# A selective scan in a Mamba and mixture-of-experts layer: GpSimd adds the two states of every second unit, TensorE adds one tile instead of two

## The chip, the cores and the metric

The kernel runs on one core of one Trainium2 chip. The metric is the device time of one launch in microseconds. Three runs of the kernel before took 6356.14, 6356.43 and 6366.62 us; their median is 6356.43 us. All tensors of the part that matters here are 32-bit floats.

## The reference, cut to what matters

```python
# per sequence, x: (512 tokens, 256); D_INNER = 512 channels, D_STATE = 16
xz = x @ in_proj_w.T;  u, res = split(xz, 2)
u = silu(conv_b + causal 4-tap convolution of u)
dt, B, C = split(u @ x_proj_w.T)
delta = softplus(dt @ dt_proj_w.T + dt_proj_b);  A = -exp(A_log)
def step(h, t):
    h = exp(delta_t[..., None] * A) * h + delta_t[..., None] * B_t[:, None, :] * u_t[..., None]
    y = einsum('bdn,bn->bd', h, C_t)         # sum over the 16 states
y = (y + u * D_skip) * silu(res);  m = y @ out_proj_w.T
# then: layer norm, an additive attention with l2 norms, a GELU feed-forward
# of width 1024, layer norms; then top-2 routing to 8 experts with a capacity,
# the experts' matmuls, and the weighted sum with a residual
```

It is applied to 32 sequences of 512 tokens. Only the sum over the states in `y` is computed in another way by the change.

## The kernel before, in words

There are three phases one after the other: `attention_phase` (the Mamba layer, the attention, the feed-forward and the routing, for 32 sequences), `expert_phase` and `combine_phase`. The change touches the first alone, which takes about 5.4 of the 6.4 milliseconds.

**Units.** The 512 channels of a sequence are four blocks of 128 partitions. A unit is one block with two of the 16 states, so a sequence has 32 units, k = 0 to 31 (`NU`), eight to a block. For unit k:
- ScalarE computes the decays `dA` = exp(delta * A), one activation for each of the two states (`decay`, L740);
- VectorE multiplies `du` = delta * u with the row B into `drive` (`drive`, L1077, 128x1024), and runs the recurrence over dA and drive into the tile `st` (`recur`, L1104, one instruction over 2 x 512 columns);
- GpSimd multiplies `st` in place with the row C (`times_c`, L528, 128x1024);
- TensorE adds the two halves of `st` into the bank `Y` by two matmuls with the identity (`add`, L912). Each 32-bit matmul is two records in the trace, so a unit is four records of L912. A block opens with one matmul that puts u * D_skip into Y (L909), and ends with VectorE's product of Y with the gate, `gate`, L1083.

`st` has four buffers (`RING`): the recurrence of unit k waits (semaphore `scan_sum`) until TensorE has added unit k-4. B_rows has two buffers and C_rows four; SyncE loads both in one order, and a load of C_rows waits for the product of four units before.

**Side stages.** Beside the scan of sequence b, every engine works on three side stages: `pre` of sequence b+1 (norm, input projection, convolution, delta), `post` of b-1 (output projection, attention, first feed-forward matmul) and `late` of b-2 (second feed-forward matmul, norms, routing, scatter to the experts). Each engine has one instruction stream in a fixed order. That order is written out by tables: a unit has three slots, so a sequence has 96, and each `at = iter((...))` lists, for the pieces of one side stage on one engine, behind which slot each comes. `run_slots` puts the scan's part of a slot first and the pieces behind it. An engine whose next piece waits does nothing else meanwhile.

Two points of a sequence serve as marks below. *idx* is L1260 on VectorE: the table of expert slots of sequence b-2 is ready, between the recurrences of units 13 and 14; GpSimd waits for it to issue eight indirect DMAs (L615). *The gate* is the L1083 of the last block of the sequence before, in front of the recurrence of unit 1: it waits for TensorE's add of that sequence's unit 31, which follows GpSimd's product of unit 31.

## Time and profile before

| | |
|---|---|
| median of three runs | 6356.43 us |
| profiled execution, its own time | 6355.55 us |
| its span | 6353.8 us |
| TensorE busy (matmul) | 5465.8 us, 86% |
| VectorE busy | 5085.4 us, 80% |
| GpSimd busy | 4353.1 us, 69% |
| ScalarE busy | 3682.9 us, 58% |
| mean granted TensorE clock | 0.933 |

The busy shares are over the whole span. The first phase takes most of it, and the steady part of that phase (1000 to 5000 us) is where the shares are read below. "Idle before" is time that an engine spent waiting in front of an instruction, with what ended the wait behind the arrow. The time of 6355.55 us is 1.75 us longer than the span, for what lies around it.

### The profile page before, as it was taken

The numbers are of one execution on the slowest core, as the hardware profiler recorded it, in microseconds if no ns is written. First come the engines' busy times: TensorE is split into PE (matmuls) and PEld (weight loads), VectorE is DVE, ScalarE is ACT, GpSimd is POOL, SyncE is SP. The second block draws the span as 40 slices with busy tenths as digits, with TensorE's granted clock in tenths as the row PEclk, the third lists the DMA queues.
The fourth block names the chain that finished last, engine by engine and source line by source line (L and its number), as shares of the span: only waits on it lengthen the run. The fifth ranks groups of instructions, "written<-read, shape, count | busy, mean of one in ns | idle before, by whom it ended". The sixth has DMA issues, their size and how long they took to land. (4 is left out here: it accounts for less than half of the span.)

```text
span 6353.8 us, 72231 instructions
## 1 busy us (share of the span) xinstructions
PE 5465.8 (86%) x17152; PEld 3037.6 (48%) x17152; DVE 5085.4 (80%) x6700; ACT 3682.9 (58%) x6370; POOL 4353.1 (69%) x2996
## 2 busy tenths in 40 slices
PE   3788988888889898888888888898888988749997
PEld 1344444444444454454444444444454454436663
DVE  4898898898988898888898899889998888712226
ACT  3566666666666666666666666666666666421113
POOL 2677777777777777777777777777777777622223
PEclk8899999999999999999999999999999999869999
DMA  7666666666666666666666666666666666403337
GB/s 263 228 227 232 227 233 226 215 230 227 230 229 225 216 226 220 226 229 226 231 229 216 212 222 223 218 216 218 219 223 217 221 226 216 156 25 123 119 111 324
DMA packets 470519, 1349.76 MB, mean 212 GB/s; under 512 B 54495, under 2 KB 161888, under 8 KB 468592
## 3 DMA queue, kind: packets, MB, share of 16 engines
q1 hardware_dynamic: 437904, 1270.68, 59.0%
q10 hardware_dynamic: 13664, 39.47, 1.7%
q0 software_dynamic: 18432, 34.17, 1.5%
q14 instruction: 374, 3.06, 0.2%
q8 instruction: 145, 2.38, 0.1%
HBM read 1206.71 MB, written 154.66 MB: 214 GB/s over the span
## 5 line engine op out<-in xcount | busy, mean ns | idle before, releaser
L528 POOL TENSOR_TENSOR st<-st,C_rows 128x1024 f32<-128x1024 f32 x1024 | 2478.0, 2426 | 519.8 <-DVE st L1104 510.4
L1104 DVE TENSOR_TENSOR_SCAN st<-dA,drive 128x1024 f32<-128x1024 f32 x1024 | 2338.5, 2284 | 247.7 <-PE y L912 110.7
L912 PE MATMUL y<-st,ident 128*128 128x512 f32 x4096 | 1970.8, 619 | 163.4 <-POOL st L528 161.1
L740 ACT ACTIVATE dA<-delta,a_neg 128x511 f32<-128x511 f32 x2048 | 1368.0, 712 | 699.9 <-DVE st L1104 691.8
L912 PEld LDWEIGHTS y<-st,ident 128*128 128x128 f32 x4096 | 794.2, 199 | 1183.9 <-issue 878.2
L1077 DVE TENSOR_TENSOR drive<-du,B_rows 128x1024 f32<-128x1024 f32 x1024 | 1259.9, 1230 | 101.1 <-DVE du L1072 21.7
L881 PE MATMUL pre_bank<-e_abs,in_w 128*128 128x512 f32 x1024 | 579.3, 706 | 84.7 <-DVE u L1054 78.0
L860 PE MATMUL post_bank<-d_w,gT 128*128 128x256 f32 x2048 | 471.8, 388 | 35.8 <-issue 35.0
L860 PEld LDWEIGHTS post_bank<-d_w,gT 128*128 128x128 f32 x2048 | 397.9, 195 | 136.1 <-issue 82.7
L615 POOL DMA_INDIRECT expert_in<-tb,idx x256 | 271.1, 1059 | 267.0 <-DVE idx L1260 195.5
L1419 POOL DMA_INDIRECT rank_rows<-O,dest_i x128 | 124.5, 973 | 381.8 <-issue 381.8
L881 PEld LDWEIGHTS pre_bank<-e_abs,in_w 128*128 128x128 f32 x1024 | 211.4, 219 | 343.1 <-issue 204.2
L1054 DVE SCALAR_TENSOR_TENSOR u<-pre_bank,conv_w,u 128x511 f32<-128x511 f32 (+2 forms) x384 | 285.6, 744 | 36.3 <-ACT u L685 27.3
L984 PE MATMUL post_bank<-F,d_w 128*128 128x512 f32 x512 | 246.1, 626 | 3.6 <-ACT gT L811 2.0
L852 PE MATMUL post_bank<-ident,tb 128*128 128x128 f32 x768 | 117.3, 302 | 143.6 <-ACT tb L643 113.1
L860 PE MATMUL post_bank<-F,gT 128*128 128x256 f32 x512 | 157.8, 477 | 90.6 <-ACT F L792 90.6
L1371 PE MATMUL bank<-XT,w 128*128 128x512 f32 x512 | 227.7, 598 | 5.3 <-ACT XT L1396 5.3
L1381 PE MATMUL bank<-w,I 128*128 128x256 f32 x1024 | 228.6, 382 | 3.3 <-issue 3.3
L984 PE MATMUL pre_bank<-F,d_w 128*128 128x512 f32 x512 | 230.2, 592 | 0.0
L860 PE MATMUL pre_bank<-out_w,u 128*128 128x256 f32 x1024 | 226.3, 379 | 2.5 <-issue 2.5
L1404 ACT ACTIVATE I<-bank 128x512 f32<-128x512 f32 x64 | 38.2, 597 | 316.5 <-PE bank L1371 316.5
L1469 DVE TENSOR_SCALAR O<-bank,w_slot 128x256 f32<-128x256 f32 x128 | 53.1, 477 | 210.3 <-PE bank L1381 210.3
(211 smaller groups left out, 8217.6 us busy)
## 6 DMA issues: line engine op xcount, KB each, us to landing
B_rows<-bc_rows SPq DMA_DIRECT2D x1024, 512.0 KB, 3.7
C_rows<-bc_rows SPq DMA_DIRECT2D x1024, 512.0 KB, 4.9
rank_rows<-zeros SPq DMA_DIRECT2D x32, 1024.0 KB, 9.0
rows<-rank_rows SPq DMA_DIRECT2D x32, 1024.0 KB, 18.6
expert_in<-gT ACTq DMA_DIRECT2D x11, 1536.0 KB, 25.5
X<-expert_in SPq DMA_DIRECT2D x32, 528.0 KB, 3.8
xin<-in_x SPq DMA_DIRECT2D x32, 512.0 KB, 6.8
xn_rows<-xin SPq DMA_DIRECT2D x32, 512.0 KB, 3.4
```

Source lines behind the costliest of these rows:

```text
L528: pool.tensor_tensor(tile[:, :, :], tile[:, :, :], bc[1][k % ROWS[1]][:, :, :], ALU.mult)\
L615: pool.indirect_dma_start(out=xe_dram, out_offset=bass.IndirectOffsetOnAxis(ap=idx[:, tile, choice:choice + 1], axis=0), in_=tb_wide[:, ti ...
L740: return act.activation(dA[k % 2][:, j, 1:L], delta[par][:, c, 1:L], ACT.Exp, scale=a_neg[:, c, n:n + 1])
L860: last = pe.matmul(banks[tile // 2][:, (tile % 2) * D:(tile % 2 + 1) * D], srcT[:, c, tile * P:(tile + 1) * P], w[:, c, :], start=c == 0, ...
L881: last = pe.matmul(RB[m % 2][:, :], in_w[:, c, m * P:(m + 1) * P], xT[:, c, :], start=c == 0, stop=c == KD - 1)
L912: last = pe.matmul(Y[:, :], ident[:, :], st[k % RING][:, j, :], start=False, stop=pair == CU - 1 and j == 1)
L984: last = pe.matmul(FB[j % 4][:, :], d1_w[:, c, j * P:(j + 1) * P], F[:, c, :], start=c == 0, stop=c == KD - 1)
L1054: dve.scalar_tensor_tensor(late, RB[c % 2][:, 0:L - 1 - j], conv_w[:, c, 2 - j:3 - j], late, ALU.mult, ALU.add).then_inc(pre_dve.did(f"con ...
L1077: dve.tensor_tensor(DR[:, :, :], DU[:, :].unsqueeze(1).to_broadcast([P, 2, L]), bc[0][k % ROWS[0]][:, :, :], ALU.mult).then_inc(scan_in.di ...
L1104: dve.tensor_tensor_scan(st[k % RING][:, :, :].rearrange("p a l -> p (a l)"), dA[k % 2][:, :, :].rearrange("p a l -> p (a l)"), DR[:, :, : ...
L1371: last = pe.matmul(MB[m][:, 0:BLK], w1[e][:, c, m * P:(m + 1) * P], XT[n % 2][:, c, :], start=c == 0, stop=c == KD - 1)
L1381: last = pe.matmul(OB[tile // 2][:, (tile % 2) * D:(tile % 2 + 1) * D], I[n % 2][:, c, tile * P:(tile + 1) * P], w2[e][:, c, :], start=c = ...
```

## The change: every second unit is added in halves by GpSimd first

For even k, `times_c` issues a second instruction behind its product: it waits for that product, adds half 1 of `st` to half 0 (128x512) and only then signals `scan_hc`. TensorE's `add` does one matmul for such a unit instead of two. Odd units are as before. All tables of the side stages have new numbers; of these the diff shows four.

```diff
+        def PAIRED(k):
+            return k % 2 == 0
...
+        scan_pair = Steps(sem("scan_pair"), [k for k in range(NU) if PAIRED(k)])
...
-                    pool.tensor_tensor(tile[:, :, :], tile[:, :, :], bc[1][k % ROWS[1]][:, :, :], ALU.mult)\
+                    product = pool.tensor_tensor(tile[:, :, :], tile[:, :, :], bc[1][k % ROWS[1]][:, :, :], ALU.mult)
+                    if not PAIRED(k):
+                        product.then_inc(scan_hc.did(k), 1)
+                        return
+                    product.then_inc(scan_pair.did(k), 1)
+                    pool.wait_ge(*scan_pair.at(k, b))
+                    pool.tensor_tensor(tile[:, 0, :], tile[:, 0, :], tile[:, 1, :], ALU.add)\
                         .then_inc(scan_hc.did(k), 1)
...
@@ gpsimd @@
             def post(b, par, more):
-                at = iter((13, 19, 22, 34, 37, 41, 53, 53, 61, 70))
+                at = iter((11, 22, 22, 36, 40, 46, 54, 55, 61, 70))
...
             def late(b):
-                at = iter((0, 1, 18, 20, 22, 27, 29, 43, 43, 45, 45, 45, 45, 48, 51))
+                at = iter((5, 7, 21, 23, 25, 25, 32, 44, 45, 46, 46, 46, 46, 46, 51))
...
-                    for j in range(2):
+                    halves = (0,) if PAIRED(k) else (0, 1)
+                    for j in halves:
                         last = pe.matmul(Y[:, :], ident[:, :], st[k % RING][:, j, :], start=False,
-                                         stop=pair == CU - 1 and j == 1)
+                                         stop=pair == CU - 1 and j == halves[-1])
...
@@ tensor @@
             def late(b):
-                at = iter((0, 10, 10, 13, 38, 38, 45))
+                at = iter((0, 7, 10, 11, 36, 40, 43))
...
@@ vector @@
             def late(b):
-                at = iter((13, 18, 18, 18, 40, 40, 42))
+                at = iter((15, 18, 21, 21, 40, 40, 41))
```

**GpSimd around idx.** In the kernel before, from the product of unit 11 to that of unit 15 (gT is the attention's `li`; the DMAs wait for idx):

```order
L528 TENSOR_TENSOR st<-st,C_rows 128x1024 [waits scan_h]
L565 REGISTER_ALU
L541 TENSOR_TENSOR gT<-gT,row_lni_g 128x1024 [waits post_act]
L526 REGISTER_ALU
L527 REGISTER_ALU [waits C_loaded0]
L528 TENSOR_TENSOR st<-st,C_rows 128x1024 [waits scan_h]
L568 REGISTER_ALU
L545 TENSOR_TENSOR gT<-gT,row_lni_b 128x1024 [waits post_pool]
L527 REGISTER_ALU [waits C_loaded1]
L528 TENSOR_TENSOR st<-st,C_rows 128x1024 [waits scan_h]
L612 REGISTER_ALU
L615 DMA expert_in<-tb,idx 16384x264 [waits late_dve]
```

In the changed kernel, from the product of unit 13 to that of unit 15:

```order
L532 TENSOR_TENSOR st<-st,C_rows 128x1024 [waits scan_h]
L622 REGISTER_ALU
L625 DMA expert_in<-tb,idx 16384x264 [waits late_dve]
L625 DMA expert_in<-tb,idx 16384x264
L531 REGISTER_ALU [waits C_loaded2]
L532 TENSOR_TENSOR st<-st,C_rows 128x1024 [waits scan_h]
L537 REGISTER_ALU
L538 TENSOR_TENSOR st<-st 128x512 [waits scan_pair]
L625 DMA expert_in<-tb,idx 16384x264 x5
L578 REGISTER_ALU
L555 TENSOR_TENSOR gT<-gT,row_lni_b 128x1024 [waits post_pool]
L531 REGISTER_ALU [waits C_loaded3]
```

The wait for idx still stands directly behind the product of unit 13. The addition of row_lni_b has moved from in front of it to behind it, and the product of unit 14 now comes behind two DMAs instead of six.

**VectorE at the feed-forward's norm.** Before, between the recurrences of units 5 and 6 (the form SCALAR_TENSOR_TENSOR of L1104 is the recurrence; the scale r_late of L1188 comes from GpSimd), from the norm's aggregation on:

```order
L1041 BN_AGGR mv_late<-stat_late 128x2 x3
L1186 REGISTER_ALU
L1188 SCALAR_TENSOR_TENSOR post_bank<-post_bank,mv_late,row_ln_g 128x256 [waits late_pool]
L1188 SCALAR_TENSOR_TENSOR post_bank<-post_bank,mv_late,row_ln_g 128x256 x3
L1191 REGISTER_ALU
```

In the changed kernel, the same place:

```order
L1052 BN_AGGR mv_late<-stat_late 128x2 x3
L1112 REGISTER_ALU
L1115 SCALAR_TENSOR_TENSOR st<-dA,drive 128x1024 [waits scan_sum,scan_in,scan_exp]
L1088 TENSOR_TENSOR drive<-du,B_rows 128x1024 [waits scan_h,B_loaded1]
L1197 REGISTER_ALU
L1199 SCALAR_TENSOR_TENSOR post_bank<-post_bank,mv_late,row_ln_g 128x256 [waits late_pool]
```

A whole recurrence and a drive now stand between what GpSimd computes r_late from and what uses it.

**ScalarE at the norm of h.** Before, from the first decay of unit 5 to the second (the normalisation of h waits for GpSimd's h_shift, the one of L656 for x_m):

```order
L740 ACTIVATE dA<-delta,a_neg 128x511 [waits scan_h]
L758 ISA
L643 ACTIVATE h<-h,shift,r 128x256 [waits post_pool]
L643 ACTIVATE h<-h,shift,r 128x256 x3
L740 ACTIVATE dA<-delta,a_neg 128x511
```

In the changed kernel, from the second decay of unit 7 to the first of unit 8:

```order
L750 ACTIVATE dA<-delta,a_neg 128x511
L686 ISA
L687 ISA [waits pre_pe]
L688 COPY e_abs<-pre_bank 128x512 [waits pre_dve]
L689 COPY e_abs<-pre_bank 128x512
L768 ISA
L653 ACTIVATE h<-h,shift,r 128x256 [waits post_pool]
L653 ACTIVATE h<-h,shift,r 128x256 x3
L749 REGISTER_ALU
L750 ACTIVATE dA<-delta,a_neg 128x511 [waits scan_h]
```

The wait for h_shift no longer stands between the two decays of unit 5; it has moved two and a half units back.

## Rows read from the trace of the kernel before

**Rows 1.** Windows: length, busy time and instructions of each engine, PEclk, DMA share, GB/s
```profile
1000.00:5000.00 4000.00, 3540.93 (x11064) 1937.47 (x11062) 3559.84 (x4441) 2600.66 (x4464) 3064.52 (x1994) 0.94 0.66 223
2028.10:2117.20 89.10, 78.47 (x204) 36.74 (x203) 77.71 (x70) 58.32 (x81) 74.88 (x42) 0.92 0.74 251
2117.20:2200.90 83.70, 73.97 (x270) 45.98 (x270) 74.03 (x120) 52.23 (x111) 55.52 (x44) 0.95 0.57 189
2200.90:2285.60 84.70, 75.50 (x208) 36.66 (x208) 78.04 (x72) 58.62 (x82) 73.67 (x42) 0.97 0.78 264
```

**Rows 2.** One line's instructions, 1000 to 5000 us: idx, and who waited
```profile
L1260 DVE TENSOR_SCALAR idx<-slot_f x24: 170/171/172, 1010.7 to 4933.0; 128x8 uint32<-128x8 f32 x24
...
  POOL expert_in L615: 144.8, 24
```

**Rows 3.** Groups by line, 1000 to 5000 us: busy us, mean ns, idle before
```profile
L528 POOL TENSOR_TENSOR st<-st,C_rows 128x1024 f32<-128x1024 f32 x752 | 1820.4, 2427 | 323.0 <-DVE st L1104 318.2
L1104 DVE TENSOR_TENSOR_SCAN st<-dA,drive 128x1024 f32<-128x1024 f32 x752 | 1717.5, 2284 | 185.1 <-PE y L912 83.0 <-ACT dA L740 45.1 <-issue 26.1
L912 PE MATMUL y<-st,ident 128*128 128x512 f32 x3004 | 1431.3, 614 | 73.0 <-POOL st L528 71.1
```

**Rows 4.** Waits of VectorE, 1000 to 5000 us: total us, times, longest
```profile
DVE st L1104 <- PE y L912: 83.0, 64, 2.9
DVE st L1104 <- ACT dA L740: 45.1, 58, 3.3
DVE post_bank L1188 <- POOL r_late L472: 36.4, 23, 1.6
DVE tb L1159 <- PE post_bank L860: 34.3, 16, 3.3
...
DVE gT L1134 <- PE post_bank L860: 11.6, 12, 1.0
DVE cum L1240 <- PE post_bank L1015: 10.6, 12, 1.3
```

**Rows 5.** Timeline of TensorE: start us, us, operation [idle before]
```profile
2078.81 1.09 PE L852 MATMUL post_bank<-ident,tb 128*128 128x128 f32 x8 [2.34 <-ACT tb L643]
2081.03 3.78 PE L912 MATMUL y<-st,ident 128*128 128x512 f32 x4 [1.13 <-POOL st L528]
...
2143.85 5.31 PE L912 MATMUL y<-st,ident 128*128 128x512 f32 x12
```

**Rows 6.** Windows: the four microseconds behind that idle time
```profile
2080.00:2084.00 4.00, 2.97 (x4) 1.43 (x5) 3.81 (x3) 2.95 (x5) 4.00 (x3) 0.50 0.77 271
```

**Rows 7.** Groups by line, GpSimd, 1000 to 5000 us: its short tensor_tensor
```profile
L482 POOL TENSOR_TENSOR shift<-shift,r 128x4 f32<-128x4 f32 x70 | 17.0, 242 | 5.5
```

**Rows 8.** Groups by line, GpSimd, 2028.9 to 2112.6 us: idx to unit 31
```profile
L528 POOL TENSOR_TENSOR st<-st,C_rows 128x1024 f32<-128x1024 f32 x18 | 44.5, 2481 | 10.7 <-DVE st L1104 10.7
L615 POOL DMA_INDIRECT expert_in<-tb,idx x8 | 8.5, 1068 | 8.8 <-DVE idx L1260 6.9 <-issue 1.9
```

**Rows 9.** Timeline of GpSimd
```profile
2028.96 1.11 POOL L615 DMA_INDIRECT expert_in<-tb,idx  x1 [6.94 <-DVE idx L1260]
...
2051.13 6.99 POOL L528 TENSOR_TENSOR st<-st,C_rows 128x1024 f32<-128x1024 f32 x3
...
2091.53 3.26 POOL L528 TENSOR_TENSOR st<-st,C_rows 128x1024 f32<-128x1024 f32 x1 [1.32 <-DVE st L1104]
...
2109.81 2.71 POOL L528 TENSOR_TENSOR st<-st,C_rows 128x1024 f32<-128x1024 f32 x1 [2.79 <-DVE st L1104]
```

**Rows 10.** Timeline of VectorE: idx, the gate, two waits behind it
```profile
2027.88 0.17 DVE L1260 TENSOR_SCALAR idx<-slot_f 128x8 uint32<-128x8 f32 x1
...
2117.27 0.68 DVE L1083 TENSOR_TENSOR u<-y,g 128x512 f32<-128x512 f32 x1
...
2140.70 2.29 DVE L1104 TENSOR_TENSOR_SCAN st<-dA,drive 128x1024 f32<-128x1024 f32 x1 [3.34 <-ACT dA L740]
...
2148.49 1.67 DVE L1188 SCALAR_TENSOR_TENSOR post_bank<-post_bank,mv_late,row_ln_g 128x256 f32<-128x256 f32 x4 [1.58 <-POOL r_late L472]
```

More of the change, by code:

```diff
@@ L370, in pre @@
             def pre(b, par):
-                at = iter((2, 16, 52, 64, 95))
+                at = iter((8, 37, 70, 71, 95))
                 yield next(at)
@@ L410, in post @@
             def post(b, par, more):
-                at = iter((4, 52))
+                at = iter((2, 68))
                 yield next(at)
@@ L425, in late @@
             def late(b):
-                at = iter((38, 58))
+                at = iter((31, 51))
                 yield next(at)
@@ L463, in _ @@
                                pattern=[[1, P]], channel_multiplier=-1).then_inc(consts, 1)
-            for steps in (pre_pool, scan_hc, post_pool, late_pool):
+            for steps in (pre_pool, scan_pair, scan_hc, post_pool, late_pool):
                 steps.credit(pool)
@@ L502, in pre @@
             def pre(b, par):
-                at = iter((11, 16, 67, 69, 70, 73))
+                at = iter((12, 17, 67, 67, 77, 89))
                 yield next(at)
@@ L660, in pre @@
             def pre(b, par):
-                at = iter((10, 14, 17, 17, 19, 19, 25, 36, 43, 43, 48, 55, 59, 59, 59, 60, 61, 62, 65, 66, 69, 92))
+                at = iter((14, 14, 17, 19, 21, 29, 34, 37, 42, 47, 47, 53, 53, 61, 64, 64, 65, 65, 67, 68, 71, 94))
                 def junk(tile):
@@ L755, in post @@
             def post(b, par, more):
-                at = iter((12, 20, 35, 35, 35, 35, 37, 53, 64, 73, 76, 86, 95))
+                at = iter((20, 23, 28, 32, 38, 38, 38, 54, 67, 80, 80, 92, 95))
                 yield next(at)
@@ L814, in late @@
             def late(b):
-                at = iter((22, 25, 25, 30, 36, 42))
+                at = iter((26, 26, 28, 32, 37, 42))
                 yield next(at)
@@ L864, in pre @@
             def pre(b, par):
-                at = iter((20, 25, 25, 25, 36, 38, 46, 46, 47, 49, 52, 52, 55, 55))
+                at = iter((16, 16, 27, 30, 36, 41, 41, 46, 46, 51, 51, 53, 55, 55))
                 yield next(at)
@@ L922, in post @@
             def post(b, par, more):
-                at = iter((1, 2, 24, 26, 26, 44, 48, 54, 61, 67, 76, 78, 83, 84, 88))
+                at = iter((0, 1, 18, 27, 33, 49, 52, 56, 63, 63, 78, 88, 88, 93, 94))
                 for half in range(2):
@@ L1044, in pre @@
             def pre(b, par):
-                at = iter((20, 28, 33, 39, 82, 88, 95))
+                at = iter((22, 33, 37, 39, 85, 95, 95))
                 for c in range(KI):
@@ L1086, in gates @@
             def gates(b, par):
-                at = iter((30, 56, 77))
+                at = iter((28, 54, 78))
                 for c in range(KI - 1):
@@ L1117, in post @@
             def post(b, par, more):
-                at = iter((2, 11, 11, 27, 31, 44, 49, 58, 68))
+                at = iter((2, 10, 11, 25, 26, 46, 51, 63, 68))
                 yield next(at)
```

## The prediction

> **What bounds the kernel now.** I read the busy shares first, then one period of the sequence loop, then who waits for whom. The reader should see that the first phase repeats one pattern: idx comes 24 times from 1010.7 to 4933.0 us [rows 2], so a sequence takes 3922.3 / 23 = 170.5 us. Such a period holds, by 1000 to 5000 us [rows 1], 151.7 us of VectorE (89.0%), 150.9 of TensorE (88.5%), 130.6 of GpSimd (76.6%) and 110.8 of ScalarE. No engine is full. The recurrence on VectorE, 2284 ns [rows 3], waits for the other three, and its waits are the time to be won: for TensorE's add 83.0 us, for ScalarE's decays 45.1, for GpSimd's r_late 36.4, for TensorE's side matmuls 34.3, 11.6 and 10.6 [rows 4]. Over 23.5 sequences (752 units of 32, [rows 3]) that is 5.9 us per sequence for TensorE, 1.9 for ScalarE and 1.5 for GpSimd.
>
> I cut the period at two marks. From idx to the gate the traced sequence takes 2117.2 - 2028.1 = 89.1 us, the next one 84.7; from the gate to idx 83.7 [rows 1, 10]. Over the 24 sequences the first part goes from 84.6 to 89.5 us with a mean of 87.3, the second from 80.3 to 88.7 with a mean of 83.2. The quick first part had a granted clock of 0.97, the slow one 0.92 [rows 1]: TensorE makes the difference between them.
>
> **TensorE's part of the change.** It loses one matmul for each of 16 units per sequence, two records each. Twelve records in a row take 5.31 us at full clock [rows 5], so 0.43 us each with the tail taken off (0.44 by plain division): 16 x 2 x 0.43 = 13.8 us per sequence, 440 us in all. None of it is on the path by itself. What it can give back is VectorE's wait for TensorE, 5.9 us per sequence, and a share of ScalarE's.
>
> **GpSimd's part.** It gains 16 additions of 128x512 per sequence. No row has this form. The bounds are the product of twice the width, 6.99 us for three, so 2.33 each [rows 9], and the 128x4 tensor_tensor, 0.24 us [rows 7]. I take the straight line between them, 0.24 + 508 x (2.36 - 0.24) / 1020 = 1.30 us, since the length grows with the columns and 512 lies in the middle. The wait for its own product adds the 0.08 us that the dependent L482 shows in front of it (5.5 us over 70, [rows 7]). With the overlap of two independent instructions lost, 1.4 us each; 22.4 us per sequence. GpSimd then has 153 us of work in 170.5, more than VectorE. Waiting behind the addition are the next product, all side pieces of GpSimd, and SyncE's load of C_rows four units on, with the B_rows load behind it in the same queue.
>
> [...]
>
> **Where it binds: from idx to the gate.** GpSimd's wait for idx stands directly behind the product of unit 13 in both kernels. From the first DMA behind it to the end of the product of unit 31, 2028.96 to 2109.81 + 2.71 = 2112.52, it took 83.6 us [rows 9], of which 10.7 us were waits for the recurrence [rows 8]. Its own work was 72.9 us, with the 0.9 and 0.35 us by which products stretch beside some of VectorE's work (3.26 and 2.71 against 2.36, [rows 9]). Now nine additions (units 14 to 30) come in, 9 x 1.4 = 12.6, and the addition of row_lni_b that was in front of idx, 2.3 us: 72.9 + 12.6 + 2.3 = 87.8 us with no wait. Before it lie 0.9 us from idx to the first DMA (2028.05 to 2028.96, [rows 9, 10]); behind it TensorE's two matmuls of unit 31, 1.8 us. So the gate comes no earlier than 90.5 us behind idx, against 87.3 now: +3.2 us per sequence. With the additions at the lower bound (0.24 + 0.08) this is 80.8 and GpSimd doesn't bind; at the upper (2.36 + 0.08) it is 99.9.
>
> VectorE's recurrences do not stop in between for long: the four buffers let them run up to four units ahead, some 15 us. But gate and recurrence of unit 1 stand behind unit 31's sum, and there the lag is collected. This is where the gain on TensorE in the same part is lost.
>
> **From the gate to idx.** Here GpSimd was busy 55.5 of 83.7 us [rows 1]; seven additions make it 65, so it has room. VectorE was busy 74.0. What goes: the 3.34 us wait for the decays of unit 5 [rows 10] stood behind ScalarE's wait for h_shift, which is now two and a half units later; the 1.58 us for r_late [rows 10] is covered by a recurrence and a drive, 3.5 us. In the mean over the sequences the two are worth 1.9 + 1.5 us. Half of TensorE's 5.9 us falls into this part; I take 1.9 of 2.9 as gone, and give 0.3 back for the new places where TensorE waits for x_normed early. Sum: 83.2 - 5.0 = 78.2 us. What is late next in this part is the chain of h_sum, h_aggr and h_shift, which starts at the gate.
>
> **The sum.** 90.5 + 78.2 = 168.7 us against 170.5, -1.8 us; 31 periods give -56 us. From the profiled execution, 6355.6 us: 6355.6 - 56 = 6300 us; the median of the runs before is 0.9 us above that execution, which I leave out. The other two phases do not change.
>
> **Rivals.**
> *GpSimd doesn't bind (faster by far).* If the additions are cheap, or overlap more than I grant, the first part becomes what it is when TensorE is in time, 84.7 us: 84.7 + 78.2 = 162.9, -7.6 x 31 = -236, 6120 us; with an addition of about 0.9 us all told, 9 x 0.5 less than mine, it is 86.0 + 78.2 = 164.2, 6160. For it: the quick sequences. Against: 15 us of new work in a part where 10.7 were free.
> *GpSimd binds and nothing is won behind the gate (slower).* The gate is late, so GpSimd comes into the next part already behind, h_shift and r_late come later, and VectorE's waits there stay as they are: 90.5 + 83.2 = 173.7, +3.2 x 31 = +99, 6455 us. For it: GpSimd at 153 of 170 us, and every wait of it now delays products. It decides if the part from gate to idx stays over 82 us. Against: GpSimd's 28 us of idle time in that part.
> *The clock takes it back (no change).* [...] TensorE with 13.8 us less to do stands still more often. If the mean clock falls from 0.94 to 0.88, its work at full clock, 150.9 x 0.94 - 13.8 = 128 us, takes 146 us, hardly less than 151: VectorE's waits for it stay, the period stays at 170.5, 6356 us. [...] Against: the new idle time lies in pieces of under a microsecond behind every second unit, and the clock stayed at 0.97 in the quick stretch, where TensorE was idle for 9 of 85 us [rows 1].
> [...]
>
> **How the numbers follow.** The forecast has 0.43, GpSimd not binding 0.17, the slow case 0.27, the clock 0.13. The measurement tells 0.2% (12.7 us, 0.4 us per sequence) from no change. The forecast's own range is 6250 to 6350, nearly all of it faster (0.37, same 0.04, slower 0.02); the first rival 0.17 faster; the second 0.25 slower, 0.02 same; the clock 0.07 same, 0.03 and 0.03. That makes faster 0.57, same 0.13, slower 0.30. The range must reach into both sides: from 6165, which leaves out the cheapest additions, to 6455, the slow case's own value; the dearest additions (99.9 + 78.2 = 178.1, 6592 us) lie beyond it.
>
> **What would show it.** The addition's row near 1.3 us x 512. TensorE's L912 with 3072 records in place of 4096, its busy share near 82%. GpSimd near 90% in the first phase, with hardly any wait for the recurrence from idx to the gate; the gate at 90 to 91 us behind idx. VectorE's wait at the gate appearing as a new row, its wait for r_late gone, for the decays under half. I am wrong if the first part is under 88 us (then the additions or the stretches are cheaper than taken), or the second over 82 (then the new places don't give what I read from them).

## The result, and the profile after

The changed kernel takes 6554.3 us (median of 4 runs, 6549.3 to 6563.0) against 6358.5 (4 runs): a ratio of 1.031 with a 95% interval of 1.029 to 1.033. The forecast was 6300 us and its range ended at 6455. Profiled span: 6550.2 us.

Windows of the changed kernel, columns as in [rows 1]: the first phase, then one sequence cut at idx and at the gate.

```profile
1000.00:5000.00 4000.00, 3328.58 (x9967) 1807.42 (x9968) 3542.67 (x4306) 2580.86 (x4388) 3413.16 (x2296) 0.87 0.65 216
2105.20:2201.40 96.20, 80.27 (x216) 41.08 (x214) 81.10 (x71) 60.10 (x82) 84.87 (x51) 0.84 0.70 238
2201.40:2281.60 80.20, 65.08 (x227) 38.48 (x226) 74.57 (x120) 53.20 (x112) 65.39 (x51) 0.92 0.58 196
```

Over the sequences of this window the period is 176.1 us for 170.5. The first part (idx to gate) has a mean of 96.1 for 87.3, the second (gate to idx) 80.0 for 83.2. TensorE's granted clock is down from 0.94 to 0.87.

Groups by line, 1000 to 5000 us, columns as in [rows 3]: GpSimd's product and addition, TensorE's sum.

```profile
L532 POOL TENSOR_TENSOR st<-st,C_rows 128x1024 f32<-128x1024 f32 x727 | 1751.8, 2415 | 154.7 <-DVE st L1115 152.1
...
L538 POOL TENSOR_TENSOR st<-st 128x512 f32<-128x512 f32 x363 | 460.2, 1268 | 28.5
...
L923 PE MATMUL y<-st,ident 128*128 128x512 f32 x2184 | 1197.0, 677 | 159.1 <-POOL st L532 121.2 <-POOL st L538 36.9
```

GpSimd's wait for the recurrence is halved, from 318 us in [rows 3] to 152, as new work fills it; TensorE's wait for GpSimd is more than doubled, from 71 to 158.

The pieces of the attention that are named below, in the order in which one needs the other: ssk (sums of squares of the keys, TensorE, then VectorE), the product with w_g (VectorE), G (TensorE) and ssg (VectorE), t (VectorE), t_li (t plus the earlier `li`, GpSimd), its transpose (TensorE) and the copies F (ScalarE), fl (TensorE's matmuls with fl_w), s_sum (fl plus h, VectorE), s_normed (ScalarE) and its transpose sT (TensorE). asg is the routing's assignment of tokens; xp_w is the product whose copy xd leads over dt to delta and so to the decays.

Waits of VectorE, columns as in [rows 4]. L1177 is s_sum (L1166 in the code before), L1164 ssg, L1155 the product of gT with w_g, L1094 the gate.

```profile
DVE tb L1177 <- PE post_bank L870: 114.3, 23, 5.7
DVE st L1115 <- PE y L923: 53.5, 41, 2.5
DVE ssg L1164 <- PE post_bank L971: 37.7, 23, 3.4
DVE gT L1155 <- PE post_bank L961: 34.5, 18, 3.5
DVE gT L1155 <- issue: 17.4, 5, 3.5
DVE u L1094 <- PE y L923: 16.0, 15, 1.8
...
DVE st L1115 <- ACT dA L750: 11.3, 30, 0.6
```

What [rows 4] had at the top is down (83.0 to 53.5 for the sum, 45.1 to 11.3 for the decays, r_late's 36.4 gone, the 34.3 at t, L1159, down to 7.3). But there are new waits at side pieces, all in the first part: 114.3 + 37.7 + 34.5 + 17.4 = 204 us, 9.0 per sequence (for the 17.4 the profile names no releaser). One of these is the longest single wait of the sequence. Timeline of VectorE, changed kernel: t, and s_sum after it.

```profile
2138.23 1.65 DVE L1170 SCALAR_TENSOR_TENSOR tb<-post_bank,rk,row_pr_b 128x256 f32<-128x256 f32 x4
...
2152.37 1.29 DVE L1177 TENSOR_TENSOR tb<-post_bank,h 128x512 f32<-128x512 f32 x2 [5.25 <-PE post_bank L870]
```

Between the two lies a chain over three engines. GpSimd's t_li ran from 2140.92, TensorE's transpose at 2143.33, ScalarE's copies F at 2145.93, TensorE's fl at 2147.03: 12.5 us from the end of t. On VectorE t stands at slot 63 where it was at 58, while s_sum stayed at 68. That is two recurrences between them in place of three, and VectorE waits for the rest. Part of this wait is TensorE's clock. Timeline of TensorE at fl, and the window over it:

```profile
2147.03 5.22 PE L870 MATMUL post_bank<-fl_w,F 128*128 128x256 f32 x16 [1.73 <-ACT F L807]
```

```profile
2147.00:2152.00 5.00, 4.97 (x16) 4.18 (x17) 0.13 (x1) 4.78 (x6) 5.00 (x3) 0.69 0.58 174
```

After idle times of 3.51 us in front of the transpose and 1.73 us in front of fl the mean granted clock over fl was 0.69: 0.50 in each microsecond from 2147 to 2150 us, 0.95 in the next and 1.00 from 2151 on. fl's 16 matmuls took 5.22 us. In the mean they take 5.3 us here, at a granted clock of 0.65 to 0.71 in each of the 23 sequences, and 3.7 in the kernel before, where it is 1.00 over all 24.

### The profile page after: what moved, and what is told of

It reads as the page before. It is cut to its first block and busy times, and to the rows that moved or that the text cites. A ratio compares the mean times of both kernels' runs of the same rounds, so it can differ in the third digit from the quotient of the medians.

```text
span 6550.2 us, 71204 instructions
## 1 busy us (share of the span) xinstructions
PE 5330.4 (81%) x16128; PEld 2945.1 (45%) x16128; DVE 5212.2 (80%) x6700; ACT 3759.7 (57%) x6430; POOL 4984.3 (76%) x3508
## 5 line engine op out<-in xcount | busy, mean ns | idle before, releaser
L923 PE MATMUL y<-st,ident 128*128 128x512 f32 x3072 | 1688.2, 680 | 271.4 <-POOL st L532 178.4
L750 ACT ACTIVATE dA<-delta,a_neg 128x511 f32<-128x511 f32 x2048 | 1353.2, 712 | 834.3 <-DVE st L1115 810.8
L923 PEld LDWEIGHTS y<-st,ident 128*128 128x128 f32 x3072 | 630.4, 214 | 1048.1 <-issue 618.9
L538 POOL TENSOR_TENSOR st<-st 128x512 f32<-128x512 f32 x512 | 649.0, 1268 | 40.2
L891 PE MATMUL pre_bank<-e_abs,in_w 128*128 128x512 f32 x1024 | 597.7, 723 | 68.1 <-ACT e_abs L689 38.3
L891 PEld LDWEIGHTS pre_bank<-e_abs,in_w 128*128 128x128 f32 x1024 | 228.7, 235 | 378.8 <-issue 237.4
L862 PE MATMUL post_bank<-ident,tb 128*128 128x128 f32 x768 | 147.6, 355 | 262.0 <-ACT tb L653 150.3
L862 PEld LDWEIGHTS post_bank<-ident,tb 128*128 128x128 f32 x768 | 119.0, 183 | 355.8 <-ACT tb L653 198.3
L919 PE MATMUL y<-u,d_diag 128*128 128x512 f32 x256 | 196.5, 860 | 100.2 <-DVE u L1094 100.2
L995 PE MATMUL post_bank<-F,d_w 128*128 128x512 f32 x512 | 232.7, 597 | 1.5 <-ACT F L814 1.5
```

The lines of the kernel that those rows point to most:

```text
L538: pool.tensor_tensor(tile[:, 0, :], tile[:, 0, :], tile[:, 1, :], ALU.add)\
L750: return act.activation(dA[k % 2][:, j, 1:L], delta[par][:, c, 1:L], ACT.Exp, scale=a_neg[:, c, n:n + 1])
L862: last = pe.transpose(banks[c][:, tile * P:(tile + 1) * P], src[:, tile, c * P:(c + 1) * P], ident[:, :])
L891: last = pe.matmul(RB[m % 2][:, :], in_w[:, c, m * P:(m + 1) * P], xT[:, c, :], start=c == 0, stop=c == KD - 1)
L923: last = pe.matmul(Y[:, :], ident[:, :], st[k % RING][:, j, :], start=False, stop=pair == CU - 1 and j == halves[-1])
L995: last = pe.matmul(FB[j % 4][:, :], d1_w[:, c, j * P:(j + 1) * P], F[:, c, :], start=c == 0, stop=c == KD - 1)
```

## The experiments

Times are given as ratios to the kernel before, measured in the same session; 1% is 64 us and the intervals are about 0.2% to either side. Parts and periods are means over the sequences of 1000 to 5000 us. "Old" and "new places" are the tables of before and of the change.

| run | ratio, 95% interval | us | first part | second part | clock |
|---|---|---|---|---|---|
| before | 1 | 6353 to 6374 | 87.3 | 83.2 | 0.94 |
| changed | 1.031 [1.029, 1.033] | 6554 | 96.1 | 80.0 | 0.87 |
| e1, new places alone | 1.038 [1.036, 1.040] | 6612 | 97.2 | 80.8 | 0.92 |
| e2, pairs alone | 1.025 [1.022, 1.027] | 6531 | 92.1 | 84.3 | 0.89 |
| e3, both matmuls | 1.042 [1.039, 1.044] | 6639 | 98.3 | 80.2 | 0.91 |
| e4, short addition | 1.018 [1.016, 1.021] | 6492 | 95.3 | 79.5 | 0.88 |
| f1, s_sum later | 1.044 [1.041, 1.047] | 6637 | 98.1 | 81.2 | 0.86 |
| f2, three steps later | 1.054 [1.051, 1.057] | 6700 | 100.4 | 80.7 | 0.86 |
| f3, pairs from unit 22, old places | 1.020 [1.018, 1.023] | 6485 | 88.7 | 86.5 | 0.91 |
| f5, du first | 1.041 [1.038, 1.043] | 6613 | 95.5 | 83.2 | 0.86 |
| g3, tail of the chain later | 1.025 [1.024, 1.027] | 6515 | 94.5 | 80.5 | 0.88 |
| g5, old chain, pairs | 1.032 [1.030, 1.034] | 6553 | 92.2 | 84.0 | 0.88 |
| g6, old chain, no pairs | 1.036 [1.034, 1.037] | 6581 | 95.2 | 82.3 | 0.94 |
| h1, routing, no pairs | 1.041 [1.039, 1.042] | 6616 | 97.5 | 80.4 | 0.92 |
| h2, routing, pairs | 1.030 [1.028, 1.031] | 6547 | 96.1 | 80.0 | 0.87 |
| h3, routing and xd, pairs | 1.035 [1.034, 1.037] | 6584 | 96.3 | 81.4 | 0.85 |
| h4, chain, routing, xd, no pairs | 1.011 [1.009, 1.013] | 6425 | 89.8 | 82.7 | 0.94 |
| k1, the same with pairs | 1.028 [1.026, 1.031] | 6540 | 92.5 | 83.8 | 0.88 |
| k2, chain and xd, no pairs | 1.018 [1.016, 1.021] | 6478 | 91.9 | 82.3 | 0.92 |
| k3, h4 with two gates later | 1.020 [1.018, 1.023] | 6488 | 88.6 | 85.9 | 0.94 |

**The two halves of the change, e1 and e2.** e1 is before.py's code with the new places; e2 is the changed kernel with the old ones:

```diff
# e1: GpSimd and TensorE as before, all tables new
-                    product = pool.tensor_tensor(tile, tile, bc[1][k % ROWS[1]], ALU.mult)
-                    ... pool.tensor_tensor(tile[:, 0, :], tile[:, 0, :], tile[:, 1, :], ALU.add)
+                    pool.tensor_tensor(tile, tile, bc[1][k % ROWS[1]], ALU.mult)
# e2: pairs, and each `at = iter(...)` as before
```

> The new tables without the pair additions: TensorE adds both halves of every unit, GpSimd issues the product alone. Theory A (the new places of the side pieces are the cause: VectorE reaches ssk, ssg and s_sum too soon behind what they wait for; 114.3 + 37.7 + 34.5 + 17.4 us of waits over 23 sequences, 8.9 us each) expects most of the loss here too: 6450 to 6550 us, with a wait of VectorE for fl's matmuls of 3 us or more per sequence. Theory B (GpSimd's 22 us of additions per sequence are the cause, the places are fitting) expects no loss: 6330 to 6370 us.

> The pair additions with the tables of the kernel before. Theory A expects little loss, since three recurrences stand between t and s_sum as before: 6350 to 6430 us, idx to the gate at 90 us. Theory B expects the loss in full or more, since the places were not fitted to it: 6550 us or more, idx to the gate at 96 us or more. Theory C (TensorE's lower granted clock, 0.87 in place of 0.94 in the steady part) expects a clock below 0.90 and 6500 us or more.

Each half alone makes the kernel slower: the places by 3.8%, the pairs by 2.5%. Together they cost 3.1%, less than the sum. e1 went the way of theory A and further than its range. e2 came out 100 us above theory A's range and inside theory C's, with a clock of 0.89; what the clock is worth follows with e3. Waits of VectorE with the new places alone:

```profile
DVE tb L1166 <- PE post_bank L860: 120.0, 22, 5.9
DVE st L1104 <- PE y L912: 71.9, 81, 2.7
DVE gT L1144 <- PE post_bank L950: 50.9, 23, 2.5
DVE ssg L1153 <- PE post_bank L960: 42.9, 23, 2.9
```

s_sum, ssk and ssg again: 213.8 us, 9.5 per sequence, and the first part is 9.9 us longer than before. No pair is in this kernel. So the places lengthen the first part, not GpSimd's additions, and they do gain in the second (80.8 for 83.2). Two parts of this price are longer work and not waits: VectorE's du takes 1260 ns in the mean for 674 before, four times per sequence (the last section shows when), and fl takes 5.5 us for 3.7. In e2 the first part is bound by GpSimd instead. Its window and, below, GpSimd's waits in it:

```profile
2094.80:2187.80 93.00, 71.50 (x185) 34.09 (x186) 78.86 (x72) 58.62 (x82) 85.83 (x51) 0.89 0.73 242
```

```profile
POOL expert_in L625 <- DVE idx L1271: 5.6, 1, 5.6
POOL expert_in L625 <- issue: 1.7, 6, 0.3
POOL st L532 <- DVE st L1115: 1.5, 2, 1.4
POOL tb L551 <- issue: 1.5, 1, 1.5
```

Of 93.0 us GpSimd has 85.8 of work and stands 1.5 us for recurrences. Of its 5.6 us of waiting for idx only the last 0.9 lie behind idx and so in this part; the two "issue" rows are 3.2. This is the floor that the forecast described, at 92.1 in the mean for 90.5. In the changed kernel's first part GpSimd had 84.9 of 96.2 us and waited 7.4 for recurrences: not the bound.

**What relief and addition are worth, e3 and e4**, each the changed kernel with one line altered. e3 keeps the additions, but TensorE adds half 1 as well, so y counts it twice; e4 adds four columns alone, so y lacks most of half 1 of every second unit.

```diff
# e3
-                    halves = (0,) if PAIRED(k) else (0, 1)
+                    halves = (0, 1)
# e4
-                    pool.tensor_tensor(tile[:, 0, :], tile[:, 0, :], tile[:, 1, :], ALU.add)
+                    pool.tensor_tensor(tile[:, 0, 0:4], tile[:, 0, 0:4], tile[:, 1, 0:4], ALU.add)
```

> The changed kernel with TensorE doing both matmuls for the even units too (the second half is then counted twice in y, by the additions' in-place result; all times are those of the work). It gives TensorE back its 13.8 us per sequence. Theory C expects the clock to come back to 0.92 or more and the time to fall, below 6500 us. Theories A and B, in which TensorE's relief was a small gain, expect the same or a loss: 6554 to 6650 us.

> The changed kernel with the addition cut to 4 columns of each half (the rest of the second half is left out of y): its semaphores and places stay, its length goes from 1.27 to about 0.24 us, 16 us per sequence less on GpSimd. Theory B expects nearly all of the loss to go: 6300 to 6370 us. Theory A expects at most a third of it to go: 6480 us or more.

e3 stands 0.4% above e1 (6639 and 6612 us in one session): there the additions alone cost 26 us. e3 stands 1.1% above the changed kernel: the matmuls left out bring some 70 us at the new places. e4 stands 1.2% below it: with 0.20 us for 1.27 per addition, some 80 us come back, and the kernel is still 1.8% slower than before with a first part of 95.3 us. The additions are thus no explanation of that part. Theories B and C are out with this: B expected 6300 to 6370 us of e4, C under 6500 of e3. The mean clock doesn't order the times: e1 and e3 have 0.92 and 0.91, the changed kernel 0.87, and both are slower than it. But in both fl is slow as in the changed kernel (5.5 and 5.7 us, at a granted clock of 0.59 to 0.71), so what the low clock in front of s_sum costs is not excluded by them.

**One close pair taken apart, f1, f2, f5** (changed kernel, slots):

```diff
# f1: s_sum and its shift
- DVE post (..., 63, 68)   POOL post (..., 61, 70)
+ DVE post (..., 63, 71)   POOL post (..., 61, 73)
# f2: f1, and w_g's product, ssg, G
- DVE post (..., 46, 51,   POOL post (..., 54, 55,
+ DVE post (..., 49, 54,   POOL post (..., 55, 55,
# f5: du and drive ahead of the side pieces beside them
- DVE pre (22, ..., 85, 95, 95)   DVE post (..., 46, ...)
+ DVE pre (23, ..., 85, 92, 95)   DVE post (..., 47, ...)
```

> The changed kernel with VectorE's s_sum at slot 71 instead of 68 (three recurrences between t and s_sum, as before the change, instead of two) and GpSimd's scale of s at 73 instead of 70. Theory A' (the new places put dependent side pieces too close together on VectorE; s_sum alone costs 5.0 us per sequence) expects the wait of s_sum to fall under 2 us and the time by 80 to 150 us: 6400 to 6475. Theory R (that wait only collects GpSimd's lag, which would show at the next recurrence or at the gate instead) expects the wait to reappear there and the time to stay: 6530 to 6570.

> As f1, and the product with w_g (it waits for ssk) at slot 49 instead of 46 and ssg at 54 instead of 51, GpSimd's power of G at 55 instead of 54. The three waits together cost 114.3 + 34.5 + 17.4 + 37.7 us over 23 sequences, 8.9 us each. Theory A' expects 30 to 80 us less than f1: 6350 to 6430. Theory R expects no gain over f1, since t and s_sum only come later with them.

> The changed kernel with three places of VectorE such that du follows a recurrence directly: the first convolution at 23 instead of 22, the product with w_g at 47 instead of 46, delta2 at 92 instead of 95. In the changed kernel du takes 1450 ns in the mean instead of 674, and delta 1618 instead of 1199: both read two tiles from SBUF while a product of GpSimd is running. Theory P (such an instruction of VectorE waits for the rest of GpSimd's, when GpSimd's began first) expects du back under 900 ns, 2 to 3 us per sequence: 6470 to 6500 us. If the durations are stretched by shared bandwidth wherever they stand, du stays at 1300 ns or more and the time at 6540 to 6570.

All three are slower than the changed kernel, by 1.3, 2.3 and 1.0%. In f1 the wait at s_sum is gone, as it should be. The first lines of TensorE's and of VectorE's waits show what stands in its place:

```profile
PE post_bank L862 <- ACT tb L653: 185.8, 22, 9.6
```

```profile
DVE st L1115 <- PE y L923: 226.8, 74, 7.5
```

sT, the transpose behind s_sum, kept its slot on TensorE. TensorE now stands up to 9.6 us in front of it, with adds queued behind, and the recurrences wait for those. The theory of a single tight pair fell. f5 was expected to bring du under 900 ns and the time to 6470 to 6500 us; du came to 1210 ns, while delta went from 1618 to 2149.

**The whole tail later, and the whole chain back, g3, g5, g6.**

```diff
# g3 (changed kernel): s_sum 71, shift 73, s_normed 82, sT 83, fl 66
# g5 (changed kernel), g6 (e1): before's places from ssk to s_sum
- DVE post (..., 46, 51, 63, 68)          DVE pre (..., 85, 95, 95)
+ DVE post (..., 44, 49, 58, 68)          DVE pre (..., 82, 88, 95)
- POOL pre (..., 67, 77, 89)
+ POOL pre (..., 69, 70, 73)
- POOL post (..., 46, 54, 55, 61, 70)     PE post (..., 49, 52, 56, 63, ...)
+ POOL post (..., 41, 53, 53, 61, 70)     PE post (..., 44, 48, 54, 61, ...)
- ACT post (..., 38, 38, 38, 54, 67, ...) ACT pre (..., 61, 64, 64, 65, 65, 67, 68, 71, 94)
+ ACT post (..., 37, 37, 37, 53, 64, ...) ACT pre (..., 59, 59, 60, 61, 62, 65, 66, 69, 94)
```

> The changed kernel with the tail of the chain moved later as one piece: s_sum on VectorE at slot 71 (for 68), its shift on GpSimd 73, s_normed and sT's copies on ScalarE 82 and 83 (for 80), fl's second step on TensorE 66, sT 83 (for 78). All computed is as in the changed kernel. When s_sum alone was moved to 71 the time went up by 82 us, with TensorE then waiting 186 us for s_normed. Theory A: that wait goes and s_sum's wait of 114 us stays away, first part about 94 (it is still tight from ssk to t), 6490 to 6530 us. Theory R: another wait comes in its place, 6550 us or more.

> The changed kernel, pairs and all, with the same chain places put back as in the run beside it. Theory A: first part from 96.1 to the 90.5 to 92 that GpSimd's work allows (92.1 with the pairs and all the old places), second part 80 to 81, period 171 to 173, 6370 to 6440 us. Theory R: first part over 94, 6520 us or more. If A holds, this run against the one beside it gives what the pairs are worth with neither chain tight: A expects them to cost 50 to 120 us there, since the first part is then bound by GpSimd.

> The new tables without the pairs (6612 us in the run of the tables alone), with the chain of the first part as a whole put back to its old places on the four compute engines: on VectorE the w_g product, ssg, t and s_sum at slots 44, 49, 58, 68 (for 46, 51, 63, 68) and the deltas at 82, 88; on GpSimd t_w, G and t_li at 41, 53, 53; on ScalarE tb behind ssk at 37, G's at 53, F at 64 and the taps from 59 on; on TensorE ssk, G, the transposes and fl at 44, 48, 54, 61. All computed is as in the kernel before. Theory A (the tight chain from ssk to s_sum is the cost of the tables, and pieces moved alone only moved the wait): the first part goes from 97.2 back to about 88 us, the second stays at 80.8, period 169 to 170, 6290 to 6350 us, below the kernel before. Theory R (no chain of its own; tables are a fit of all side pieces to each other, and a mixed one has waits elsewhere): first part over 94, 6500 us or more.

g3 came out inside theory A's numbers: s_sum's wait is gone and the first part is 94.5 us, though VectorE's wait for TensorE's sum rose from 53.5 to 81.8 us. The same move of s_sum that cost 1.3% in f1 gains 0.6% once s_normed, sT and fl move with it. g5 gave nothing (6553 us for the expected 6370 to 6440): its first part fell to 92.2 us as expected, but the second grew from 80.0 to 84.0. g6 refuted A's larger claim: the waits for ssk, ssg and s_sum are down from 214 to 31 us, du is back at 700 ns and fl at 3.7 us, and only 0.2% came back, no more than the intervals. Most of what went came back as one wait, VectorE's for the decays (33.3 us in e1, 184.9 in g6); another 41 us came at its gates (26.8 and 68.0). Timelines of VectorE and ScalarE in g6:

```profile
2131.06 2.29 DVE L1104 TENSOR_TENSOR_SCAN st<-dA,drive 128x1024 f32<-128x1024 f32 x1 [7.33 <-ACT dA L740]
```

```profile
2127.80 0.58 ACT L698 COPY xd<-pre_bank 48x512 f32<-48x512 f32 x1 [8.41 <-PE pre_bank L887]
2128.40 1.28 ACT L740 ACT_TABLE_LOAD   x1
2129.69 0.72 ACT L740 ACTIVATE dA<-delta,a_neg 128x511 f32<-128x511 f32 x1
```

ScalarE stood 8.41 us for TensorE's xp_w product with the next decays queued behind xd. In the new places xd is at slot 47 and the product at 51 (before: 48 and 49). In e1 ScalarE stood as long there (176.5 us, 194.3 in g6), while VectorE waited only 33.3 us for decays: it was late itself, from its waits for TensorE.

**Which group is late first, h1 to h4, k2.** Two more candidates: xd, and TensorE's routing matmuls, moved from slot 45 to 43 ahead of an add. The waits of ScalarE at xd and of TensorE for asg, before and in e1:

```profile
ACT xd L698 <- PE pre_bank L887: 60.0, 24, 3.8
...
PE post_bank L1013 <- DVE asg L1231: 3.5, 11, 0.4
```

```profile
ACT xd L698 <- PE pre_bank L887: 176.5, 23, 9.5
...
PE post_bank L1013 <- DVE asg L1231: 98.7, 23, 4.4
```

```diff
# routing: h1 (e1), h2 (changed kernel)
- PE late (..., 40, 43)   DVE late (..., 40, 41)
+ PE late (..., 40, 45)   DVE late (..., 40, 42)
# xd: h3 (on h2); h4 (on g6, with routing); k2 (on g6, without routing)
- PE pre (..., 46, 51, 51, 53, 55, 55)   ACT pre (..., 47, 47, 53, ...)
+ PE pre (..., 47, 49, 52, 52, 55, 55)   ACT pre (..., 47, 50, 53, ...)
```

> The new tables without the pairs (6612 us in the run of the tables alone; first part 97.2 us, second 80.8), with one piece put back: TensorE's matmuls on the routing's assignment, which wait for VectorE's asg, at slot 45 (before's place) in place of 43, and VectorE's use of them at 42 (before's) in place of 41. All computed is as in the kernel before. Theory Q (the tables put that piece of TensorE ahead of an add, so that TensorE stands still until VectorE has done the routing, 4.3 us per sequence, and everything queued behind it, add, g, ssk, xp_w, comes late): the wait of TensorE for asg goes from 98.7 us to under 10, the first part to 92 to 94, 6450 to 6540 us. Theory R (no single place; the wait comes back behind another piece): first part over 95.5, 6570 us or more.

> The changed kernel, pairs and all, with the same two numbers put back (TensorE's routing matmuls at slot 45 for 43, VectorE's use at 42 for 41). All computed is as in the changed kernel. There TensorE waits 82.8 us for asg, 3.6 per sequence. Theory Q: that wait goes, first part from 96.1 to 92.5 to 94.5, 6450 to 6510 us. Theory R: 6530 us or more.

> As the run beside it (pairs, routing matmuls at 45), and the step from TensorE's xp_w product to ScalarE's copy xd taken apart again: TensorE's g3, xp_w and the four dt matmuls at 47, 49, 52, 52, 55, 55 (before's; the changed kernel has 46, 51, 51, 53, 55, 55), ScalarE's xd at 50 for 47. In the changed kernel ScalarE stands at xd for 153 us in 1000 to 5000 us with the decays of the next units queued behind it; before it was 60. All computed is as in the changed kernel. Theory Q: another 1 to 3 us of the first part go, 6400 to 6480 us. Theory R: no better than the run beside it by more than 10 us.

> The new tables without the pairs, with the old places of the chain ssk to s_sum (6580 us in the run of these), of the routing matmuls, of xp_w and dt, and xd at 50. All computed is as in the kernel before. In the run with the chain alone VectorE waited once per sequence, 7.4 us, for the decays that stood behind xd, and TensorE 100.5 us for asg. Theory Q (routing, xd and chain are the cost of the tables, together): first part 86 to 89 us, 6290 to 6380 us. Theory R: over 6480 us.

> The new tables without the pairs, with the chain and xp_w, dt and xd put back, but TensorE's routing matmuls left at 43. All computed is as in the kernel before. The chain alone gave 6580 us, with xd and routing 6425. Theory C with xd as the chain next in line (VectorE waited 7.4 us per sequence for the decays queued behind it): 6430 to 6470 us, so the routing place is worth 5 to 45. Theory Q' (the routing wait of TensorE, 100 us, is what makes xd late): over 6530 us.

The routing place alone gives nothing, without pairs (1.041 for 1.038) or with them (1.030 for 1.031). It didn't take its own wait away either: TensorE still waits 60.3 us for asg in h1, where under 10 were expected. Routing and xd with the chain left tight cost 0.4%, in the changed kernel (h3, 1.035); without pairs this was not run, nor was xd alone. Yet the three groups together take e1 from 1.038 to 1.011: the first part falls from 97.2 to 89.8 us. Built up one by one, without pairs: chain 0.2%, then xd 1.7% (k2, 8 us above theory C's range), then routing 0.8%. So the groups act together, as theory Q has it. But h4's expected 6290 to 6380 us were missed: some 70 us of the places' cost are left over. Of these the profile shows a part that no run takes away. Timelines of h4, TensorE and VectorE, at the end of a first part:

```profile
2129.56 3.60 PE L984 MATMUL post_bank<-F,d_w 128*128 128x512 f32 x8
2133.00 3.60 PE L984 MATMUL pre_bank<-F,d_w 128*128 128x512 f32 x8
2136.43 5.31 PE L912 MATMUL y<-st,ident 128*128 128x512 f32 x12
```

```profile
2141.78 0.69 DVE L1083 TENSOR_TENSOR u<-y,g 128x512 f32<-128x512 f32 x1 [2.00 <-PE y L912]
```

The last matmuls of the feed-forward stand at TensorE's slots 93 and 94 (before: 84 and 88), directly ahead of the last sums, and VectorE waits at the gate: 80 us over the 23 sequences of h4, 3.5 each, where it waited nothing before. g6, k2 and k3 have 65 to 69 us there. Putting these matmuls back was not tried.

**The pairs when the places have room, k1, and one wait less, k3.** k1 is the changed kernel with all three groups; k3 is h4 with

```diff
- DVE gates (28, 54, 78)
+ DVE gates (30, 56, 78)
```

> The changed kernel, pairs and all, with the three groups of places put back together as in the run at 6425 us: the chain ssk to s_sum, TensorE's routing matmuls at 45, xp_w and dt with xd at 50. All computed is as in the changed kernel. Theory C (several chains of the first part end at about the same time, so that only all of them together give time back; then the first part falls on GpSimd's own 90.5 us): first part 91 to 93, second 81 to 83.5, 6390 to 6470 us; against the 6425 without pairs they are then worth between -35 and +45 us, no longer the 58 us that they gained with the tight places. Theory R (pairs and places each add their own cost): 6554 - 190 = 6364 us or less.

> The kernel of the 6425 us run (no pairs, three groups of places put back) with VectorE's first two gates also at before's slots, 30 and 56 for 28 and 54. All computed is as in the kernel before. There VectorE waited 39.3 us at the second gate for TensorE's sum, 1.7 per sequence. Theory C: that wait goes and first part ends at 88 to 89, 6370 to 6410 us. Theory R: the wait moves to the gate at the end of the part, 6415 us or more.

k1 is far above what either theory gave: the pairs cost 1.7% there (1.028 for 1.011), and the places that gain 2.7% without pairs gain 0.3% with them. In a first part of 91.7 us (2275.8 to 2367.5) GpSimd has 84.4 us of work and 3.2 of waiting for recurrences, close to the floor of e2 (85.8 and 1.5). Against h4 the first part is 2.7 us longer and the second 1.1. Against the changed kernel the first is 3.6 us shorter and the second 3.8 longer: VectorE waits there, 74.2 us in all, for ScalarE in front of a conv tap, where the changed kernel has no such wait. g5 and e2 trade the two parts in the same way, with periods of 176.1 and 176.3 us; why is not shown. k3 is 0.9% slower than h4. It took the wait at the second gate away (39.3 us) and shortened the first part by 1.2 us; the second grew by 3.2, with VectorE waiting 51.3 us for decays (19.2 in h4) and 87.5 for a conv tap (49.8). Why two slots at two gates do this is not shown.

**Fewer pairs, f3**: old places, pairs only in the even units from 22 on.

```diff
-            return k % 2 == 0
+            return k % 2 == 0 and k >= 22
```

> The tables of the kernel before, and the pair addition only for the five even units from 22 to 30, where GpSimd waited for the recurrence in the kernel before and TensorE had the feed-forward's matmuls as a backlog. By the account of GpSimd's work from idx to the gate (10.7 us free, 1.4 us for an addition) five additions fit with 3.7 us left, and TensorE gets 4.3 us per sequence back where VectorE waited 1 to 3.5 us for it: faster than before, 6290 to 6350 us. If any lag on GpSimd costs as much as in e2 (165 us for 16 additions), it is 6400 us or more.

Expected were 6290 to 6350 us. Five pairs in place of sixteen still cost 2.0%: 1.4 us in the first part and 3.3 in the second, though no addition stands in the second. VectorE waits 53.1 us there (12 times, up to 6.0) at h's pieces for TensorE. No version came below the kernel before.

## Why the prediction was wrong

**The step that failed** is the value of the first part: "the gate comes no earlier than 90.5 us behind idx", then used as what it would be. It is a floor for GpSimd alone, and a fair one (92.1 and 92.5 in e2 and k1, where GpSimd hardly waits). The working gave the new places no price in that part. They cost 9.9 us per sequence by themselves (e1), and the forecast's +3.2 became +8.8. Times 31 sequences the missing 5.6 us are 174 of the 254 us between forecast and result. The second part, below, has 1.8 x 31 = 56 of the rest; the other 24 are in neither.

None of the two signs of being wrong that the prediction named came true (a first part under 88, a second over 82): it didn't look for a first part that is too long. What did differ from its list of signs is the gate at 96.1 us for 90 to 91, GpSimd at 85% for near 90, and its 7.4 us of waits for recurrences from idx to the gate, where hardly any were expected.

**How the places cost this** is shown by runs, not by one wait. At least three chains in that part end close together: ssk to s_sum, the one from the routing, and the one from g over xp_w and xd to the decays. Each was drawn tighter: s_sum 5 slots behind t for 10, the routing matmuls ahead of an add, xd 4 slots ahead of its product for 1. Each engine works its queue in order: in g6 ScalarE stood 8.41 us at xd, and the recurrence 7.33 us for the decays queued behind it. So I take it that the latest chain sets VectorE's lateness and hides the others, and that is how I read it that removing one (h1, g6) returns nothing clear of the intervals and moving a piece of one (f1) costs. e1, g6, k2 and h4 walk down that stair: 1.038, 1.036, 1.018, 1.011. How the cost divides between the chains depends on the order in which they are removed.

**The second part**: 78.2 us forecast, 80.0 measured; the direction and the two reasons are right. r_late's wait is gone, the decays' fell to a quarter, and e1 (80.8) shows that the places do it. Mis-sized is the 1.9 us for TensorE's relief: measured against e1 all that the pairs add there is 0.8. The places were to give 3.1 and gave 2.4.

**The addition**: 1.27 us and 0.08 of wait, where 1.30 and 0.08 were taken. TensorE's records are 3072 and its share 81% (82 forecast), with 3328.6 x 0.87 / 22.7 = 128 us per sequence at full clock, as forecast. GpSimd's work is 3413.2 / 22.7 = 150 us per sequence for 153.

**The rivals.** "GpSimd binds and nothing is won behind the gate" had the side right and the mechanism wrong: the second part is under 82 us and GpSimd doesn't bind. It is right in kind for the pairs alone: e2 has 92.1 + 84.3, 1.025. "The clock takes it back" had its clock right (0.88 forecast, 0.87), but the mean clock is not what sets the time: g6 has the 0.94 of before and is 3.6% slower. Locally it does cost, 1.6 us at fl. The dip of [rows 6] is of the same kind: at 0.50 four records of L912 took 3.78 us [rows 5], where the four from 2074.48 us on, at 1.00, took 1.98. The pairs cost 2.5% at the old places and 1.7% at the mended ones, where GpSimd is then left with 1.5 and 3.2 us of waiting for recurrences in the first part. They gain 0.7% at the tight ones, where GpSimd had 14.8 us of such waits without them (e1, 2119.1 to 2216.4).

**What could have been read before.** The chain behind t had no room left. Timelines of the kernel before, VectorE's t and s_sum, and TensorE's fl:

```profile
2054.41 1.66 DVE L1159 SCALAR_TENSOR_TENSOR tb<-post_bank,rk,row_pr_b 128x256 f32<-128x256 f32 x4 [2.12 <-PE post_bank L860]
...
2069.98 1.28 DVE L1166 TENSOR_TENSOR tb<-post_bank,h 128x512 f32<-128x512 f32 x2
```

```profile
2065.87 3.72 PE L860 MATMUL post_bank<-fl_w,F 128*128 128x256 f32 x16 [0.84 <-ACT F L797]
```

fl ended at 2069.59, 0.4 us before s_sum needed it, with three recurrences in between. In the mean s_sum came 13.5 us behind the end of t with a wait of 0.07. With a recurrence and a drive fewer, 2.28 + 1.23 us, no such chain can be in time: by these rows alone at least 3 us of wait per sequence. The mean became 12.2 us with a wait of 5.0, of which 1.6 us are fl's own stretch from 3.7 to 5.3.

Left open: what the last 1.1% of the new places is beside the wait at the gate (h4), why the second part loses with the pairs what the first gains (g5, k1), and why f3's and k3's small edits lengthen the second part by over 3 us.

## What to carry to other kernels

Where a table sets the order of several in-order queues, price every pair of producer and consumer whose distance shrinks: the chain's length from the trace against the work left between the two places, before counting what the change saves. When mending one wait moves nothing, look for the chain that ends just behind it and move both; the two groups that were put back alone, without pairs, gave 0.2% and -0.3%, and with the third 2.7%. And before moving work to an engine with idle time, look whether its waits lie in the stretch where the work arrives: the same pairs went from -0.7% to +2.5% with the places around them.

## What the runs showed of the hardware

Two kinds of VectorE instructions that read both operands from SBUF, du and delta, took longer when they began under an instruction of GpSimd on 128x512 or 128x1024: in the changed kernel du 2.24 us for 0.68 and delta 2.06 for 1.20, in the mean. The timeline of the changed kernel, VectorE and then GpSimd:

```profile
2189.46 2.06 DVE L1070 SCALAR_TENSOR_TENSOR delta<-delta,e_abs 128x1024 f32<-128x1024 f32 x1
2191.56 2.73 DVE L1083 TENSOR_TENSOR du<-delta,u 128x512 f32<-128x512 f32 x1
```

```profile
2189.18 1.27 POOL L538 TENSOR_TENSOR st<-st 128x512 f32<-128x512 f32 x1
2190.39 3.34 POOL L532 TENSOR_TENSOR st<-st,C_rows 128x1024 f32<-128x1024 f32 x1
```

du, 0.67 us in the kernel before, takes 2.73 and ends 0.6 us, about its own length, behind the product (2194.3 and 2193.7). The product began while delta was running, and takes 3.34 for 2.36. Over 1000 to 5000 us of the changed kernel 45 of the 91 du began under such an instruction and took 2.24 us in the mean, and each of them ended 0.55 to 0.56 us behind it; the other 46 took 0.68. Of the 45 delta 22 began under an addition, took 2.04 to 2.07 us and ended 1.08 us behind it; the other 23 took 1.20. `drive` has its first operand in PSUM: 515 of 726 began so, and none took over 1.23 us. Over all, du has a mean of 1450 ns for 674 before, and delta 1618 for 1199. With 4 and 2 of them per sequence that is 3.9 us of VectorE time, which no row of waits shows and to which the forecast gave no price. What in the hardware does this is not shown.
